# Rotary angles computed during the load of x, positions fetched second, and two roundings moved to ScalarE

## The reference

```
x = x + slot_attention(layernorm(x))               # 16 heads, 64 slots
x = x + cross_attention(layernorm(x), ctx, pos)    # 32 heads of 8, rotary angles from pos
x = x + experts(layernorm(x))                      # 8 experts, the best 2 of them, and a shared one
```

## Time and profile before

| | |
|---|---|
| time, median of 3 runs | 603.45 us (602.92 to 604.12) |
| the profiled execution | 603.6 us, of which its span is 601.8 |
| TensorE busy, matmuls | 575.6 us, 96% |
| VectorE busy | 485.0 us, 81% |
| ScalarE busy | 371.2 us, 62% |
| GpSimd busy | 281.9 us, 47% |
| DMA | 19.34 MB, 32 GB/s over the span |

### The profile page before, as it was taken

How to read it: one execution, slowest core, us unless ns; L and a number is a source line. 1 busy time by engine, 2 the same in 40 slices (tenths; PEclk the granted TensorE clock), 3 DMA queues, 4 the chain that set the end, 5 groups by cost and what they waited for, 6 DMA issues and landing times. The chain is left out here.

```text
span 601.8 us, 14128 instructions
## 1 busy us (share of the span) xinstructions
PE 575.6 (96%) x4426; PEld 486.0 (81%) x4426; DVE 485.0 (81%) x1150; ACT 371.2 (62%) x1168; POOL 281.9 (47%) x324
## 2 busy tenths in 40 slices
PE   5989999999999999999999999998789999999997
PEld 5868888888888888888888788886568878877786
DVE  6999978977977986987987798677587887887766
ACT  3438557657657567556655576676867567567453
POOL 3367754845764663764575566355762211210000
PEclk9999999999999999999999999999999999999999
DMA  8200201100200200200200000232000000000000
GB/s 277 71 0 5 85 0 36 54 2 10 78 0 0 87 0 0 87 0 0 83 4 0 19 3 1 89 92 103 3 3 11 3 11 11 3 11 11 4 10 17
DMA packets 10096, 19.34 MB, mean 32 GB/s; under 512 B 2112, under 2 KB 5696, under 8 KB 9920
## 3 DMA queue, kind: packets, MB, share of 16 engines
q1 hardware_dynamic: 10048, 18.73, 9.2%
HBM read 17.55 MB, written 1.05 MB: 31 GB/s over the span
## 5 line engine op out<-in xcount | busy, mean ns | idle before, releaser
L884 ACT ACTIVATE sa_v<-bank 128x256 f32<-128x256 f32 x64 | 24.5, 382 | 60.8 <-PE bank L268 60.8
L857 ACT ACTIVATE sa_ex<-sa_okb,sa_minus_top 128x64 f32<-128x64 f32 x128 | 42.9, 340 | 28.7 <-DVE sa_minus_top L750 26.7
L947 POOL TENSOR_TENSOR sa_qt<-sa_rope_cos,sa_rope_sin 128x512 f32<-128x512 f32 x32 | 41.1, 1286 | 39.1 <-DVE sa_rope_sin L798 38.1
L266 PE MATMUL bank<-ht_hi,sa_qk_hi 128*128 128x512 f32 x128 | 55.2, 432 | 1.3 <-DVE sa_gate L803 0.9
L947 POOL TENSOR_TENSOR sa_kt<-sa_rope_cos,sa_rope_sin 128x512 f32<-128x512 f32 x32 | 41.2, 1286 | 26.6 <-DVE sa_rope_sin L798 26.6
L266 PE MATMUL bank<-sa_vg_hi,ht_hi 128*128 128x512 f32 x128 | 53.0, 414 | 0.5 <-DVE sa_rope_sin L798 0.5
L268 PE MATMUL bank<-sa_vg_hi,ht_lo 128*128 128x512 f32 x128 | 50.5, 395 | 0.0
L267 PE MATMUL bank<-sa_vg_lo,ht_hi 128*128 128x512 f32 x128 | 50.5, 395 | 0.0
L268 PE MATMUL bank<-ht_hi,sa_qk_lo 128*128 128x512 f32 x128 | 50.5, 394 | 0.0
L796 DVE TENSOR_TENSOR sa_rope_cos<-bank,con 128x512 f32<-128x512 f32 x64 | 43.9, 686 | 7.9 <-PE bank L268 6.8
L267 PE MATMUL bank<-ht_lo,sa_qk_hi 128*128 128x512 f32 x128 | 50.2, 392 | 0.0
(11 more groups left out here) (207 smaller groups left out, 1830.1 us busy)
## 6 DMA issues: line engine op xcount, KB each, us to landing
sa_qk_raw<-in_wqk SPq DMA_DIRECT2D x8, 512.0 KB, 3.8
sa_vg_raw<-in_wvg SPq DMA_DIRECT2D x8, 512.0 KB, 3.3
sa_wo_raw<-in_wo SPq DMA_DIRECT2D x8, 256.0 KB, 2.6
xf_w_raw<-in_w SPq DMA_DIRECT2D x2, 640.0 KB, 9.0
xf_w_raw<-in_w SPq DMA_DIRECT2D x1, 1152.0 KB, 7.4
xs<-in_x SPq DMA_DIRECT2D x2, 512.0 KB, 4.7
hn<-in_w SPq DMA_DIRECT2D x2, 512.0 KB, 4.6
out<-xs SPq DMA_DIRECT2D x8, 128.0 KB, 1.7
```

The costliest lines, as they stand in the source:

```text
L266: pe.matmul(out, w_hi, m_hi, start=first, stop=False)
L857: ins = act.activation(ex[:, s, u, :], okb[:, s, u, :], ACT.Exp, bias=minus_top[:, s, u:u + 1], accum_out=total[:, buffer_of(i, g, 4), u:u ...
L947: pool.tensor_tensor(dst[:, h, c * HALF:(c + 1) * HALF], rope_cos[:, s, :], rope_sin[:, s, :], ALU.add).then_inc(roped, 1)
```

## The change

- The positions are fetched second, ahead of the constants and the second half of x.
- VectorE computes the angles between the statistics of the first and of the second half of x, instead of ahead of VG 0. It waits for the constants before them.
- ScalarE loads the table with the sine at its very start, takes the sine before anything else, and loads the table with exp and tanh ahead of the list `H_ACT`. The step RS goes.
- RT comes first in VectorE's list, in place of RA, and not between VG 4 and QK 2.
- The two roundings of u (the CASTs of line 725) become copies on ScalarE; VectorE makes both halves of `u_full` first, then both subtractions. TensorE's ST and SN wait for 2 instead of 4 counts, since only the subtractions count now. VG 0's gate, which overwrites `u_full`, waits for both.

```diff
-H_DVE = [("RA", 0, -1), ("VG", 0, -1), ("VG", 1, -1), ("QK", 0, -1), ("QK", 1, -1), ("VG", 2, -1), ("VG", 3, -1),
-    ("SN", 0, -1), ("SN", 1, -1), ("VG", 4, -1), ("RT", 0, -1), ("QK", 2, -1), ("QK", 3, -1), ("VG", 5, -1),
+H_DVE = [("RT", 0, -1), ("VG", 0, -1), ("VG", 1, -1), ("QK", 0, -1), ("QK", 1, -1), ("VG", 2, -1), ("VG", 3, -1),
+    ("SN", 0, -1), ("SN", 1, -1), ("VG", 4, -1), ("QK", 2, -1), ("QK", 3, -1), ("VG", 5, -1),
...
-H_ACT = [("VG", 0, -1), ("VG", 1, -1), ("VG", 2, -1), ("VG", 3, -1), ("RS", 0, -1), ("W2P", 0, -1), ("VG", 4, -1),
+H_ACT = [("VG", 0, -1), ("VG", 1, -1), ("VG", 2, -1), ("VG", 3, -1), ("W2P", 0, -1), ("VG", 4, -1),
...
-    def vector_stats(self, dve, x_in):
-        for half in range(2):
+    def vector_stats(self, dve, x_in, halves=range(2)):
+        for half in halves:
...
         sp.dma_start(xs[:, 0:4, :], a["x"][0:4].rearrange("b t d -> t b d")).then_inc(x_in[0], 16)
+        sp.dma_start(rotary.pos[:, :, :], a["pos"].rearrange("b t p -> t b p")).then_inc(rotary.pos_in, 16)
         sp.dma_start(con[:, :], a["constants"]).then_inc(con_in, 16)
         sp.dma_start(xs[:, 4:8, :], a["x"][4:8].rearrange("b t d -> t b d")).then_inc(x_in[1], 16)
-        sp.dma_start(rotary.pos[:, :, :], a["pos"].rearrange("b t p -> t b p")).then_inc(rotary.pos_in, 16)
...
-                        pe.wait_ge(us_done, 4)
+                        pe.wait_ge(us_done, 2)
...
-        norm.vector_stats(dve, x_in)
+        norm.vector_stats(dve, x_in, (0,))
+        dve.wait_ge(con_in, 16)
+        rotary.vector_angles(dve)
+        norm.vector_stats(dve, x_in, (1,))
         norm.vector_norm(dve, 0)
         norm.vector_norm(dve, 1)
...
             dve.tensor_scalar(u_full[:, cols], banks[4 + half][:, :], con[:, C_ONE:C_ONE + 1], None, ALU.add).then_inc(u_full_done, 1)
-            dve.wait_ge(u_full_done, half + 1)
-            dve.tensor_copy(us[:, cols], u_full[:, cols]).then_inc(us_done, 1)
-            dve.wait_ge(us_done, 2 * half + 1)
+        for half in range(2):
+            cols = slice(half * HALF, (half + 1) * HALF)
+            dve.wait_ge(us_hi_done, half + 1)
             dve.scalar_tensor_tensor(out=us[:, cols], in0=us[:, cols].bitcast(F32), scalar=con[:, C_LOW_U:C_LOW_U + 1],
                                      in1=u_full[:, cols], op0=ALU.mult, op1=ALU.add).then_inc(us_done, 1)
...
                     dve.wait_ge(th_done, 8 * r + n + 1)
+                    if isinstance(r, int) and r == 0 and n == 0:
+                        dve.wait_ge(us_done, 2)
...
         act.sem_inc(wo_hi_done, 1)
+        act.preload_act_table_set("trig_and_small")
+        rotary.scalar(act)
         act.wait_ge(con_in, 16)
...
+        for half in range(2):
+            cols = slice(half * HALF, (half + 1) * HALF)
+            act.wait_ge(u_full_done, half + 1)
+            act.activation(us[:, cols], u_full[:, cols], ACT.Copy).then_inc(us_hi_done, 1)
+        act.preload_act_table_set("exp_and_others")
         act.wait_ge(ws2_done, 1)
```

More of the change, by code:

```diff
@@ L452, in slot_attention @@
     qk_hi_done, qk_lo_done, vg_hi_done, vg_lo_done = sem("qk_hi_done"), sem("qk_lo_done"), sem("vg_hi_done"), sem("vg_lo_done")
-    u_ready, u_full_done, us_done = sem("u_ready"), sem("u_full_done"), sem("us_done")
+    u_ready, u_full_done, us_hi_done, us_done = sem("u_ready"), sem("u_full_done"), sem("us_hi_done"), sem("us_done")
     es_hi_done, es_lo_done, tri_done = sem("es_hi_done"), sem("es_lo_done"), sem("tri_done")
@@ L809, in run @@
                     dve.tensor_scalar(dst[:, n, :], ps[:, :], -CLAMP, CLAMP, ALU.max, ALU.min).then_inc(draining, 1)
-        return every_turn(dve, H_DVE, run, banks, {"RA": lambda: rotary.vector_angles(dve), "RT": lambda: rotary.vector_tables(dve)})
+        return every_turn(dve, H_DVE, run, banks, {"RT": lambda: rotary.vector_tables(dve)})
     def scalar(act):
@@ L917, in run @@
                         act.preload_act_table_set("exp_and_others")
-        return every_turn(act, H_ACT, run, banks, {"RS": lambda: rotary.scalar(act)})
+        return every_turn(act, H_ACT, run, banks)
     def gpsimd(pool):
```

## The result

| | before | changed |
|---|---|---|
| median of 22 runs each | 604.42 us (602.92 to 605.66) | 605.30 us |
| ratio, with its 95% interval | | 1.002 [1.0011, 1.0029] |
| profiled span, granted clock | 601.8, 0.996 | 602.7, 0.996 |

What follows compares the result with a forecast made beforehand. It took the head as bound by x's landing and normalisation to 14.5 us, TensorE to 35.4, then VectorE. From 603.45 measured (603.6 profiled), 0.40 late start less 0.42 waiting gave -0.02: 603.5 us, range 602.6 to 604.9.

Steps and rivals of the forecast that it cites:

- The sum: Whole kernel: TensorE starts 0.40 us later and 0.42 of its waiting goes, net -0.02, giving 603.5 us.
- a late start of 0.40: Head of the kernel: second statistics, and with them TensorE's first projections, 0.29 to 0.48 us late; 0.40 taken.
- 0.42 won at QK 5: TensorE's wait at 36.43 us shrinks from 0.85 to about 0.43; VectorE's 0.88 relief is capped by VG 6's tanh.
- The positions, fetched second: Load queue at the start: positions ahead cost up to 0.46 us of transfer; constants by 6.24, x by 8.22 us.
- the end of the angles past the gap: VectorE before the second statistics: angles run from 6.05 to 8.05 us, the gap ends at 7.76, so 0.29 late.
- the forecast's upper bound of 0.48: Second statistics on VectorE start at 8.24 us at the latest, 0.48 late, with constants landing at 6.24 at worst.
- my 2 to 3.7: VectorE's two CASTs of u, moved to ScalarE: 2 to 3.7 us for both, the lower end likelier.
- (a): Angles' multiplications and GpSimd's first power lock each other out of a port; TensorE 1.29 late, net 0.87, 604.4 us; chance 0.15.
- (b): SyncE's 1.42 us issue behind the positions moves ahead of x; x lands at 9.68, net +1.50, 605.0 us; chance 0.13.
- (c): All relief of VectorE is used: TensorE's whole 1.73 us of waiting goes, no late start, 601.9 us; chance 0.07.
- (d): Shift takes away or brings a TensorE stretch at 1.2 GHz, at most 2.4 us either way; chance 0.05, 0.03 slower.
- The range: Forecast time of 602.6 to 604.9 us, leaving out (b), (c) and (d).

Runs made afterwards that it cites:

- h3: Changed kernel, SyncE issuing Ws1 and all loads behind it only once the first half of x has landed; single execution 602.91 us, clock 1.000.
- h4: Changed kernel, SyncE issuing the second half of x and all loads behind it only once the first half has landed; single execution 602.93 us, clock 1.000.
- f2: Kernel before, with the 0.5 KB of the slot norm's weights issued second instead of ninth; single execution 604.62 us.
- e2: Changed kernel, with the positions laid out in memory as 128 pieces of 64 bytes instead of 1024 of 8; ratio 1.0018 to the kernel before.
- e4: Changed kernel, with the two roundings of u back on VectorE; ratio 1.0012 to the kernel before.
- g4: Changed kernel, with the positions issued by ScalarE's own queue beside the first half of x; ratio 1.0005 to the kernel before.
- h2: Changed kernel, with the tanh of VG 6 ahead of the exp of SN 0 on ScalarE; ratio 1.0008 to the kernel before.
- i1: h1 with ScalarE's first order restored, the exp of SN 0 ahead of the tanh of VG 6; ratio 0.9996 to the kernel before.
- h1: Kernel before, loads unmoved; roundings and sine on ScalarE, angles on VectorE, in the 18 to 22 us wait; VG 6's tanh before SN 0's exp; ratio 0.9986, repeated 0.999.
- g2: Kernel before, with the 0.5 KB of the norm's weights issued first, ahead of the first half of x; single execution 603.92 us.
- f1: Changed kernel, with the constants issued second and the positions third; ratio 1.0012 to the kernel before.
- f4: Kernel before, with the two roundings of u on ScalarE and the positions issued behind all other loads; ratio 1.0008 to the kernel before.

## Why the prediction was wrong

The sum was -0.02: a late start of 0.40 against 0.42 won at QK 5. Measured: a late start of 1.32 against 0.38.

- **The step that failed** is the size of the term in "The positions, fetched second": constants "at 5.24 to 5.70, plus up to 0.54 ... 6.24 at worst". They came at 7.10, and TensorE started 1.32 late instead of 0.40. I had priced the positions by one slice of 1 us, 0.46 us of transfer; the dip lasts 1.2 to 1.5 us, and the sums by 4.8 us put it at 275 KB, 0.71 us at 385 GB/s. The second error was to treat the loads as strictly one behind the other: the second half of x takes its share while the constants still wait for bytes (0.82 us between h3 and h4, of which 0.49 is beyond the scatter). The positions are not the load with the smallest pieces either, as I wrote: the norm's weights come in 4 bytes, and in f2 they do the most. In the earlier trace rows the constants landed 2.5 us ahead of x and hid this.
- **The late start taken apart**: 1.33 = 0.29 + 0.34 + 0.70. The 0.29 is the end of the angles past the gap, as worked out, and their 2.00 us was right. 0.34 is the first half of x, 4.58 for 4.24, a term that I had put at nothing without a reason (the 1024 pieces; e2 takes it away). The rest is VectorE's wait for the constants, 0.60 in its row, and the overlap of successive starts. The first two terms alone pass the forecast's upper bound of 0.48: in e4, g4 and h4 VectorE waits for no constants at all, and the second statistics still start at 8.50 or 8.51, 0.74 late.
- **The gain was right in mechanism and size.** VectorE's relief was capped by the tanh of VG 6, and the wait went from 0.85 to 0.47 (0.43 forecast). h2 and i1 show the cap from both sides.
- **The roundings** are hidden in the changed kernel: e4 has the same wait with them on VectorE. They cost 2.28 us there, within my 2 to 3.7.
- **Everything from 46 us on** stands nearly as before, shifted by 0.90; TensorE idles 0.24 us more in these 339.
- **The base.** My 603.5 rests on three runs of the kernel before. On the base of 22 runs the same working gives 604.4, and the range moved along would reach from 603.6 to 605.9, over the measured 605.3. But the cost that I had put at nothing is 0.8 to 1.0 on either base, and the step above is wrong on both.

**The rivals.** (a) The port, 604.4, has the right side and almost the right size (net 0.87) for the wrong reason, which is luck: the eight multiplications took 0.68 beside GpSimd's power, which ran from 6.62 for 1.01, so nothing was locked out. Yet h1 shows the lock elsewhere: there one of the eight took 0.79 us, the others 0.15, and the first ended when GpSimd's long subtraction (16.27, 2.66) did. By the Trainium skill's rule (SBUF — State Buffer, Who interferes with whom) both should have been held; the trace agrees for the subtraction and not for the power on 4 columns, and the measurement decides. The CAST that the prediction counts for the rule is no case of it as put there, since it reads one SBUF tile and not two. (b) The stall of SyncE's issue, 605.0: its time was nearest to the result, but only through the shift of the base (its net cost was 1.50), and its mechanism did not occur. The 1.42 us did not move ahead of x, x did not land at 9.68; the statistics started at 9.09 because of the angles. (c) needed the whole wait to go and no late start: that is another kernel than the change, h1, and there it gave 0.73 and not 1.73, since the three waits behind that of QK 5 (0.19, 0.47, 0.21) moved but stayed (0.25, 0.46, 0.22). (d) The clock was the same in both profiles.

**The range** was missed by 0.4, less than the base moved. Its bounds on the landings were too narrow all the same, because they came from the rows of one order of loads; a bound "6.24 at worst" for an order never seen had nothing behind it but my reading of a queue.

## What to carry to other kernels

A load that the first instructions wait for belongs directly behind the load that is under way; a small one ahead of it costs far more than its bytes, here 0.5 KB as much as 8 KB (one profile for the 0.5 KB). Work to be hidden fits better in a gap that nobody waits at the end of (18 to 22 us here) than in one that ends with the next stage's input. And where relief on one engine buys less than it should, look for the next wait on the same instruction, here a tanh behind an exp: swapping two entries of a list took another 0.47 off the wait, where everything in the change together took 0.38.

## What the runs showed of the hardware

- When a small load (0.5 or 8 KB) has its turn in the stream, the rate falls for 1.2 us or more: 67 to 265 GB/s in the slices where it is 294 to 413 without one. Issued ahead of everything (g2) it makes no such dip and costs about its issue.
- The same kernel's runs differ with the clock granted in them: the fit over all kernels has 2.55 us per 0.01 of the mean. One place where it is lost lies ahead of the experts. View of stretches, then TensorE's timeline, of the changed kernel:

```profile
430.00:440.00 10.00, 7.09 (x45) 5.35 (x43) 5.05 (x16) 7.52 (x20) 4.17 (x6) 0.83 0.02 3
```

```profile
434.31 0.56 PE L1456 MATMUL bank<-con,hn 128*128 128x128 f32 x2 [2.41 <-DVE hn L1563]
434.65 1.91 PE L1361 MATMUL bank<-con,xf_stack 128*128 128x128 f32 x8
```

  The same of h3, whose clock was 1.000 throughout:

```profile
430.00:440.00 10.00, 6.85 (x49) 4.92 (x50) 6.19 (x23) 8.74 (x23) 3.89 (x5) 1.00 0.02 4
```

```profile
434.00 0.41 PE L1457 MATMUL bank<-con,hn 128*128 128x128 f32 x2 [2.41 <-DVE hn L1564]
434.25 1.04 PE L1362 MATMUL bank<-con,xf_stack 128*128 128x128 f32 x8
```

  In both TensorE had been idle for 2.41 us. In the one it then ran partly at the 1.2 GHz level (eight matmuls in 1.91 us), in the other at 2.4 (1.04). Why the one fell and the other did not is not shown.
- In f1 TensorE ran at half pace after 1.26 us of idling, six turnings of the unit matrix taking 1.49 us (0.82 at that point in the kernel before), while the clock column says 1.00. h4 idled for 1.10 at the same point, f4 for 1.78, and neither did. That stays open. The column is no witness there: it also says 1.00 from 8.7 to 10.2 us of the kernel before, where six turnings take 1.49 us too.
